# Bias halves ahead of the first head's maxima, and that head's scores two by two behind the value products, in the long expert bodies

## The reference

```python
def _expert(xf, mask, ...):            # H = 8 heads of D = 64
    h = _ln(xf, ln1_w, ln1_b)
    q, k, v = jnp.split(h @ ipw.T + ipb, 3, axis=-1)      # per head
    scores = q @ k.T / sqrt(D), masked to the expert's rows
    o = softmax(scores) @ v
    x1 = xf + o @ opw.T + opb
    return x1 + gelu(_ln(x1, ln2_w, ln2_b) @ w1.T + b1) @ w2.T + b2
out = sum over both choices and all experts of mask * weight * _expert(...)
```

## Time and profile before

| what | us |
|---|---|
| median of 3 runs | 1327.05 |
| the profiled execution | 1324.23 |
| its span | 1322.5 |
| PE busy | 1046.1 (79%) |
| DVE busy | 741.1 (56%) |
| ACT busy | 455.0 (34%) |
| POOL busy | 322.1 (24%) |

### The profile page before, as it was taken

The page is one execution under the profiler, slowest core; times in us unless marked ns, Lnnn a source line. Parts: engine busy times, 40 slices in busy tenths (PEclk is TensorE's granted clock), DMA queues, the critical chain, the costliest instruction groups (busy, mean ns, idle before and its releaser), DMA issues.

```text
span 1322.5 us, 19279 instructions
## 1 busy us (share of the span) xinstructions
PE 1046.1 (79%) x5070; PEld 576.6 (44%) x5071; DVE 741.1 (56%) x1573; ACT 455.0 (34%) x843; POOL 322.1 (24%) x298
## 2 busy tenths in 40 slices
PE   1986799998800888778876959979799899989984
PEld 1654467777800333434333424434344344533333
DVE  5395435441461478736784473674856636736854
ACT  1301121221312366225635314434435451235522
POOL 3102324441367144203441020000000124213311
PEclk9987799998555998989897889999999999989998
DMA  5291000000427115121323020000000312120010
GB/s 148 66 285 50 1 2 0 0 0 1 157 60 233 75 48 164 42 78 32 128 85 120 1 63 1 1 0 0 0 0 3 110 48 75 41 70 1 1 31 33
DMA packets 32650, 74.58 MB, mean 56 GB/s; under 512 B 6253, under 2 KB 6551, under 8 KB 32297
## 3 DMA queue, kind: packets, MB, share of 16 engines
q1 hardware_dynamic: 24269, 55.97, 13.6%
q0 software_dynamic: 8000, 15.44, 4.0%
q10 hardware_dynamic: 288, 2.10, 0.4%
HBM read 50.63 MB, written 24.13 MB: 57 GB/s over the span
## 4 chain that ended last, share of the span: by engine, by line
PE 63%; DVE 16%; issue 10%; ACT 5%; POOL 3%; DMA 1%; DVEq 1%; SPq 0%; ACTq 0%; POOLq 0%
PE bank L1334 16%; PE bank L1425 9%; PE bank L1207 8%; PE bank L1246 5%; PE bank L1455 3%; DVE den L2159 3%; PE bank L1510 3%; PE bank L1242 2%; PE bank L1410 2%; PE bank L1389 2%; PE bank L1412 2%; PE bank L1173 2%; POOL lists L658 1%; PE bank L1469 1%; PE bank L1229 1%
## 5 line engine op out<-in xcount | busy, mean ns | idle before, releaser
L1425 PE MATMUL bank<-probs_t,v_head 128*128 128x512 f32 (+1 forms) x288 | 146.9, 593 | 17.0 <-ACT probs_t L991 16.4
L1789 DVE TENSOR_SCALAR oh_src<-iota,edge 125x1250 f16 x178 | 101.2, 568 | 105.4 <-PE bank L1207 100.5
L2072 DVE TENSOR_REDUCE mx<-bank 128x1 f32<-128x512 f32 x144 | 88.2, 656 | 75.7 <-PE bank L1389 74.9
L991 ACT ACTIVATE probs_t<-bank 128x512 f32<-128x512 f32 x144 | 81.6, 574 | 142.3 <-PE bank L1412 130.1
L560 POOL TENSOR_TENSOR w<-w_stage,w 128x1024 f16<-128x1024 f32 x40 | 85.8, 2158 | 145.9 <-ACT w L804 145.8
L1207 PE MATMUL bank<-oh_src,oh_dst 125*125 x534 | 110.8, 357 | 2.8 <-issue 0.4
L1510 PE MATMUL bank<-probs_t,v_head 128*128 128x128 f32 (+2 forms) x192 | 88.8, 549 | 6.9 <-ACT probs_t L1042 5.1
L1334 PE MATMUL bank<-hT,w 128*128 128x256 f16 (+1 forms) x552 | 89.5, 326 | 1.9 <-DVE hT L2005 1.9
L1207 PEld LDWEIGHTS bank<-oh_src,oh_dst 125*125 x534 | 70.2, 142 | 43.5 <-issue 24.2
L1455 PE MATMUL bank<-hT,w 128*128 128x512 f16 x288 | 72.7, 385 | 7.8 <-ACT t L1016 7.8
L1334 PE MATMUL bank<-w,hT 128*128 128x512 f16 x264 | 68.0, 415 | 10.3 <-DVE hT L2005 10.3
(11 more groups left out here) (306 smaller groups left out, 1956.3 us busy)
## 6 DMA issues: line engine op xcount, KB each, us to landing
w_stage<-in_ew_dram SPq DMA_DIRECT2D x40, 512.0 KB, 3.6
lists<-zeros SPq DMA_DIRECT2D x1, 10340.0 KB, 50.2
x_in<-lists SPq DMA_DIRECT2D x20, 517.0 KB, 6.7
x_mem<-lists SPq DMA_DIRECT2D x3, 1024.0 KB, 6.2
x_mem<-lists SPq DMA_DIRECT2D x1, 2560.0 KB, 10.8
out_dram<-x_mem SPq DMA_DIRECT2D x10, 250.0 KB
big<-in_x_dram SPq DMA_DIRECT2D x10, 224.0 KB
x_mem<-in_x_dram SPq DMA_DIRECT2D x1, 2240.0 KB
```

The source lines that it names most:

```text
L991: nc.scalar.activation(probs_t[:, x % NPB, 0:cn], stb[x % 2][:, 0:cn], ACT.Exp).then_inc(s_exp, 1)
L1425: nc.tensor.matmul(pvb[(hd * nq + s) % 2][:, 0:cn], v_head[:, hd, kt, :], probs_t[:, (hd * nx + i) % NPB, 0:cn], start=(k == 0), stop=(k = ...
L1789: nc.vector.tensor_scalar(oh_src[:, bass.ds(slot, 1), i, 0:N].rearrange("p a n -> p (a n)"), iota[:, :], edge[:, 0, i, bass.ds(g, 1)], Non ...
L2072: nc.vector.tensor_reduce(mx[:, hd, t, s:s + 1], sbk[i % 2][:, 0:cn], AX.X, ALU.max).then_inc(s_mx, 1)
```

## The change

Two edits, both in the `else` bodies. On PE the scores of head 0 begin behind value 1 and not behind value `nt // 2`, and they are spread evenly: with ten tiles and 18 rows, two behind each of the nine values (before: groups of 3, 4, 3, 4 and 4 behind values 5 to 9). On DVE `bias_halves` stands between `split_pair` and the maxima of head 0 and not behind the second head's copies. No instruction is added or removed, and no DMA moves in its queue.

```diff
@@ PE @@
                     pe.wait_ge(s_mk, e * 64 + 64)
-                    late = max(2, nt // 2)
                     for t in range(1, nt):
                         value(t)
-                        if t >= late:
-                            for i in range((t - late) * nx // (nt - late), (t + 1 - late) * nx // (nt - late)):
-                                scores(0, i)
+                        for i in range((t - 1) * nx // (nt - 1), t * nx // (nt - 1)):
+                            scores(0, i)
@@ DVE @@
                     split_pair()
+                    bias_halves()
                     for i in range(nx):
                         maximum(0, i)
                     owners(e, nt)
                     second_head_copies()
-                    bias_halves()
```

## The result

The changed kernel takes 1318.04 us (median of 11 runs, 1308.38 to 1321.51), the kernel before 1325.61 (median of 11, 1321.62 to 1328.79): ratio 0.9937, 95% interval 0.9915 to 0.9958. So it is faster, by 7.6 and 10 us between the medians; the forecast gain was 13.2. The forecast time was 1313.8 in 1309 to 1318, and the median lies 0.04 us beyond the upper end. It was worked out from the first three runs' 1327.05, 1.4 above the median of all eleven. The profiled execution took 1318.69 us, its span 1317.0; before, 1324.23 and 1322.5.

A forecast was written before the change was run, and what follows sets the result against it. TensorE bounds the kernel (63% of the chain), so gains must shorten its waits. Bias halves 10.3 us plus early scores 2.9 give 13.2 at L1389, taking the 1327.05 median to 1313.8 us, 8 in 10 within 1309 to 1318.

The forecast's parts named there:

- First pair: First two early scores, behind value 1 in the ten-tile body: they wait for all splits, loss 0.4 us.
- Second pair: Next two scores, behind value 2: the second waits for a maximum that follows the bias halves on VectorE, loss 0.3 us.
- The negated maxima: First head's negated maxima on VectorE: near 775.1 us instead of 779.09, 4.0 us earlier.
- TensorE's chain: Turned scores at 777.4 us, first probability product at 779.2, which alone would put L1389 at 784.4 to 786.5.
- VectorE held by GpSimd: Six `owners` operations each held by one GpSimd operation until about 784.7 us; six copies then end at 787.5.
- Rival A: VectorE's small operations slip past GpSimd's short copies: L1389 gains 14.3 to 16.4 us, total 1311 to 1313; chance 12%.
- Head 1's first score: Second head's first score (L1389), the mark everything was summed to: from 800.82 to 787.6 us, 13.2 us earlier.
- the sentence behind the sum: After L1389, TensorE's order, the loop and next expert stay the same; loads and weight pieces move along, total 1311.0 us profiled.
- The prediction's own sign against it: A difference from the kernel before that grows or shrinks by over 2 us after 800 us would show it wrong.
- Rival B: TensorE's new stop of 1 to 3 us ahead of L1389 lowers its clock: 1.5 to 2.1 us lost, 1315.3 to 1315.9; 12%.
- rival C: First head's exponentials wait for something else until 792.8 us: only 0 to 2.9 us gained, 1324 to 1327; chance 3%.
- D: Early scores make values wait for VectorE, and later heads meet the clock at another phase: some 1334 us; chance 3%.

The follow-up runs named there:

- stop_filled: Changed kernel plus 8 unused TensorE products of 512 columns just ahead of the first score of each pair's second head; one time, 1317.3 us.
- copies_in_gaps: Changed kernel with the owners and the second head's six copies made in VectorE's gaps between the maxima; 1314.93 us, ratio 0.9913 to the kernel before.

## Why the prediction was right, and where it was short

Read from value product 1 (746.46 before, 749.80 after):
- First pair, forecast loss 0.4: the score of 752.81 waits 0.25 for the last split, 3.01 behind value 1's start. Second pair, forecast loss 0.3: 0.80 instead of 0.60 for two, so 0.2. No wait for a maximum after that; before there were 8, of 3.6 us. Right.
- Value 9's end, forecast 27.52 behind value product 1, is 27.42 (777.22). The negated maxima, forecast 28.6, are at 28.52 (778.32).
- TensorE's chain: the first probability product was forecast at 32.7 and is at 32.55.
- VectorE held by GpSimd, copies' end forecast at 41.0: 40.60 (790.40). The held ones were not six of six: L2010 and L2013 were held by the short copies, L2012 slipped between them (0.16 us), and a seventh, the first copy (785.90, 2.38 us), was held by the last piece instead, so that five copies and not six were left behind it. The Trainium skill, SBUF — State Buffer, section Who interferes with whom, has it that GpSimd's only ports are the pair that it shares with VectorE, that the pair is an exclusive lock, and that the order of issue decides who blocks. This trace agrees, short copies (0.7 us) included. Rival A, slipping through, is out.
- Head 1's first score, forecast 13.2 us earlier: 13.6. The sum up to the mark was right, to 0.4 us; the 0.4 is that copy.

The step that failed is the sentence behind the sum, that behind the mark all stays the same. The prediction's own sign against it, a difference that shrinks by over 2 us after 800, was met: it shrank by 4.8. Rival B, held at 12%, is what happened: the stop of 2.02 us brought a stretch at 1.2 GHz and took 1.7 us, within its forecast of 1.5 to 2.1; `stop_filled` and `copies_in_gaps` show it. Its argument against B was the length of the stop and some 8 us of work before it. That work was there, from 780.55 to 788.5, but its first 3.3 us ran at the lower clock. To the last projection another 0.8 goes to the clock: in the next pair TensorE stops for 3.35 us, as before (3.34), and then the clock is low for longer. The windows start 52.8 us behind pair 2, first in the kernel before, then in the changed one:
```profile
876.60:886.60 10.00, 7.46 (x20) 3.15 (x21) 5.75 (x11) 1.33 (x3) 0.00 (x0) 0.83 0.00 0
```
```profile
868.00:878.00 10.00, 7.67 (x17) 3.06 (x18) 5.38 (x11) 1.19 (x2) 0.00 (x0) 0.66 0.00 0
```
This 0.8 does not follow from the 2 us stop: `copies_in_gaps`, which has no such stop, takes 168.3 us from pair 2 to the last projection, both parts 168.1, the kernel before 167.3. And 2.3 us go in the way, for a reason that is in part open (above). So 13.6 - 1.7 - 0.8 - 2.3 = 8.8 us, between the measured 7.6 and 10. The prediction had no term for the 0.8 and the 2.3. That the time still came out beside its range, and not well above it, owes to the width that rival B and the spread of the runs had given the range: in that part luck. In the pair of profiles the start of the body adds 3.34, hence 5.5 us between the spans. Neither rival C (no gain) nor D (slower) has anything left, though D named the right lever, the granted clock of the later stages, with far too large a price for it.

## What to carry to other kernels

A wait that holds an engine is worth what the next wait in that queue allows: ask who comes second, and add only up to there. Put small operations of VectorE where GpSimd is idle; beside its long pieces each costs a whole piece (2.0 to 2.2 us here for one of 0.2). On TensorE a removed wait that leaves a shorter stop can keep part of its price as a lower clock (1.7 us here behind a stop of 2.0), so fill or remove the rest as well, and judge a gain of a few us by more than one profile.

## What the runs showed of the hardware

Beside GpSimd's pieces of 2.1 us, VectorE's operations on ten elements took 2.04 to 2.16 us, and 0.17 to 0.23 where GpSimd was idle. A stop of 2.0 us, behind 8 us of work of which the last 4.7 ran at a granted clock of 1.00, was enough for a stretch at 1.2 GHz, in all four profiles that have it. A stop of 0.33 in its place was not, nor one of 1.51 in the next pair of the kernel before (1.00 in 874:878). In one profile each, four unused products of 0.86 us in all made the way to the end 4.3 us shorter than without, and eight made it as long as none. One kernel's profile began the same stage 4.0 us apart in two executions, and its runs on one chip spread from 1320.58 to 1331.13.
